# GpSimd's angles of the self-attention in the first attention stage instead of the second, their sine and cosine on ScalarE in the first stage's tail

## The reference

```python
x = x + _L0_xattn_ref(_layernorm(x), ctx_1024, W_q, b_q, W_kv, b_kv, W_o, b_o, pos_q, pos_k)
x = x + _L0_attn_ref(_layernorm(x), w_qkv, w_o, log_scale)
x = x + _L0_ffn_ref(_layernorm(x), router_w, router_bias, gate_w, up_w, down_w, ...)

def _L0_attn_ref(x, w_qkv, w_o, log_scale):
    ...
    scale = jnp.exp(log_scale)
    pos = jnp.arange(n, dtype=jnp.float32)
    theta = pos[None, None, :, None] * INV_FREQ[None, None, None, :] * scale[None, :, None, None]
    cos, sin = (jnp.cos(theta), jnp.sin(theta))
    q = _rotate(q, cos, sin)
    k = _rotate(k, cos, sin)
    ...
```

## Time and profile before

| | us |
|---|---|
| median of 3 runs (lowest, highest) | 1844.99 (1841.77, 1850.14) |
| the profiled execution | 1842.28 |
| its span, first to last instruction | 1840.8 |
| mean granted clock of TensorE | 0.968 |

### The profile page before, as it was taken

The page is one execution under the profiler, slowest core; times in us unless marked ns, Lnnn a source line. Parts: engine busy times, 40 slices in busy tenths (PEclk is TensorE's granted clock), DMA queues, the critical chain, the costliest instruction groups (busy, mean ns, idle before and its releaser), DMA issues.

```text
span 1840.8 us, 21317 instructions
## 1 busy us (share of the span) xinstructions
PE 1698.3 (92%) x8556; PEld 1131.3 (61%) x8556; DVE 1356.2 (74%) x1095; ACT 854.0 (46%) x1083; POOL 684.0 (37%) x323
## 2 busy tenths in 40 slices
PE   5589999999999996999999999999985998999998
PEld 4377777777777763333333333333565986888886
DVE  5579999999899997999898898898752553222222
ACT  3312222222222221877888888888731644333332
POOL 3266655666655653995000000000040004444442
PEclk7789999999999999999999999999997989999999
DMA  4634444344454338444444444455339003334441
GB/s 156 200 108 153 167 160 149 126 135 163 150 168 140 103 121 203 116 103 104 115 115 115 115 115 123 109 124 120 90 92 273 3 1 108 128 124 128 128 123 57
DMA packets 73905, 231.62 MB, mean 126 GB/s; under 512 B 8924, under 2 KB 9180, under 8 KB 62992
## 3 DMA queue, kind: packets, MB, share of 16 engines
q1 hardware_dynamic: 72768, 227.39, 42.8%
q10 hardware_dynamic: 1040, 2.88, 0.6%
HBM read 150.45 MB, written 59.84 MB: 114 GB/s over the span
## 4 chain that ended last, share of the span: by engine, by line
PE 56%; POOL 17%; DMA 8%; DVE 8%; issue 7%; ACT 4%; SPq 1%; POOLq 0%; ACTq 0%; DVEq 0%
PE PS L589 12%; PE PS L618 11%; PE PS L113 8%; PE PS L114 7%; PE PS L115 7%; DMA cs<-kr 6%; POOL kr L453 4%; POOL kr L450 4%; POOL cs L451 4%; POOL kl L464 4%; PE PS L371 3%; DVE mpart L375 2%; PE PS L871 2%; DVE acc L607 1%; PE PS L628 1%
## 5 line engine op out<-in xcount | busy, mean ns | idle before, releaser
L375 DVE TENSOR_REDUCE mpart<-PS 128x2 f32<-128x1024 f32 x512 | 584.3, 1220 | 57.0 <-PE PS L371 57.0
L607 DVE TENSOR_TENSOR acc<-acc,P 128x2048 f32<-128x2048 f32 x216 | 507.5, 2417 | 42.4 <-ACT P L595 42.4
L595 ACT ACTIVATE P<-PS 128x1024 f32<-128x1024 f32 x512 | 495.1, 1025 | 91.9 <-PE PS L589 66.7
L371 PE MATMUL PS<-kh,Qbd 128*128 128x512 f32 x1024 | 323.1, 397 | 25.6 <-ACT kh L462 13.1
L618 PE MATMUL PS<-P,qe 128*32 128x512 f32 x2048 | 272.9, 606 | 0.0
L371 PEld LDWEIGHTS PS<-kh,Qbd 128*128 128x128 f32 x1024 | 190.6, 190 | 82.5 <-DVE mpart L375 21.5
L108 POOL TENSOR_TENSOR w3l<-qk,w3h 128x2048 fp32r<-128x2048 f32 x2 | 9.1, 4564 | 491.5 <-ACT w3h L105 491.5
L108 POOL TENSOR_TENSOR El<-We,Eh 128x1536 fp32r<-128x1536 f32 x36 | 126.2, 3504 | 166.3 <-ACT Eh L105 166.3
L450 POOL TENSOR_TENSOR kr<-kr,cs 128x512 f32<-128x512 f32 x64 | 82.5, 1290 | 228.6 <-DMA cs<-kr 228.6
L1018 DVE TENSOR_TENSOR hf<-sg,PS 128x512 f32<-128x512 f32 x36 | 24.8, 688 | 192.8 <-PE PS L115 189.6
L438 ACT COPY cs<-PS 128x512 f32<-128x512 f32 x64 | 37.6, 590 | 239.8 <-PE PS L115 239.8
(11 more groups left out here) (206 smaller groups left out, 2734.4 us busy)
## 6 DMA issues: line engine op xcount, KB each, us to landing
kh<-kscr SPq DMA_DIRECT2D x129, 256.0 KB, 4.2
We<-in_w_e SPq DMA_DIRECT2D x36, 768.0 KB, 6.0
y<-in_y SPq DMA_DIRECT2D x16, 1024.0 KB, 4.8
cs<-kr SPq DMA_DIRECT2D x32, 512.0 KB, 6.3
vscr<-cs SPq DMA_DIRECT2D x16, 1024.0 KB, 4.3
kscr<-kh SPq DMA_DIRECT2D x16, 1024.0 KB, 4.3
kscr<-kl SPq DMA_DIRECT2D x16, 1024.0 KB, 4.3
qe<-vscr SPq DMA_DIRECT2D x64, 256.0 KB, 4.8
```

Of the source, the lines that this page charges most:

```text
L371: ins = nc.tensor.matmul(PS[:, 2 * b + t, :], Qbd[:, h, qt * 128:(qt + 1) * 128], kh[c % 2][:, g, :], start=True, stop=True)
L375: maxfree[b] = DV.sig(nc.vector.tensor_reduce(mpart[:, 4 * (h % 4) + g, 2 * qp:2 * qp + 2, c], PS[:, 2 * b:2 * b + 2, :], AX, ALU.max))
L595: expm[s, pr] = spfree[b] = AC.sig(nc.scalar.activation(P[s % 4][:, 2 * pr:2 * pr + 2, :], PS[:, 2 * b:2 * b + 2, :], ACT.Exp, scale=SCALE))
L607: accm[s] = DV.sig(nc.vector.tensor_tensor(a[:, :, :], a[:, :, :], P[s % 4][:, :, :], ALU.add))
```

## The change

The memory of `ang`, `nn`, `cosv` and `sinv` becomes one buffer `pool_of` of 6144. After chunk 0 has begun it holds `ks`, `vo` and the angles' three work tiles, so that `cs2` is free during the first stage. The exponential of the scales moves ahead of the first sines. The positions are loaded in iteration 0, behind the query's parts. GpSimd's operations are put in a list; `pr2` is computed in iteration 1, and after `rope_done` three operations of the list follow in each iteration from 1 on, until it is empty (thirteen times three and one). ScalarE takes the sines and cosines in the tail, and both old places disappear.

```diff
-        ks, vo = cs2[:, 0, :, :], [cs2[:, 1, :, :]]
+        pool_of = sbx("pool_of", [128, 6144])
+        ang, nn, cosv, sinv = [pool_of[:, 1536 * i:1536 * i + 1536] for i in range(4)]
+        ks, vo = [pool_of[:, 2048 * i:2048 * i + 2048].rearrange("p (g n) -> p g n", g=4) for i in range(2)]
+        pr2, tm2, n2 = [pool_of[:, 4096 + 512 * i:4608 + 512 * i] for i in range(3)]
+        ex = sbx("ex", [128, 4])
...
+        AC.wait(t_const)
+        t_ex = AC.sig(nc.scalar.activation(ex[:, :], cst[:, 4:8], ACT.Exp))
         AC.wait(t_ang)
...
+        angle_ops = []
+        for g in range(4):
+            a = cs2[:, 1, g, :]
+            angle_ops.append((nc.gpsimd.tensor_scalar, a, pr2, ex[:, g:g + 1], None, ALU.mult))
+            angle_ops.append((nc.gpsimd.tensor_scalar, n2, a, INV2PI, MAGIC, ALU.mult, ALU.add))
+            angle_ops.append((nc.gpsimd.tensor_scalar, n2, n2, MAGIC, None, ALU.subtract))
+            for part in (P2A, P2B, P2C):
+                angle_ops.append((nc.gpsimd.tensor_scalar, tm2, n2, part, None, ALU.mult))
+                angle_ops.append((nc.gpsimd.tensor_tensor, a, a, tm2, ALU.subtract))
+            angle_ops.append((nc.gpsimd.tensor_scalar, a, a, 3.1415925, -3.1415925, ALU.min, ALU.max))
+
+        def angles(n):
+            for _ in range(min(n, len(angle_ops))):
+                op, *args = angle_ops.pop(0)
+                t_ang2 = PL.sig(op(*args))
+                PL.wait(t_ang2)
+            return PL.last()
...
-                        AC.wait(v_out.get(c - 1))
+                        AC.wait(v_out.get(c - 1), t_cscr, t_qrot)
...
                         t_qbd, t_qout = query_parts()
+                        SP.wait(t_qrot, t_cscr)
+                        t_pos = l_a.dma(SP, n2, A["c_pos"].to_broadcast([128, 512]))
...
                 rope_done[c] = PL.sig(nc.gpsimd.tensor_tensor(kl[:, :, :], kr[:, :, :], ...
+                if c == 1:
+                    PL.wait(t_pos, t_ex, t_qrot, t_wks)
+                    PL.wait(PL.sig(nc.gpsimd.tensor_scalar(pr2, n2, cst[:, 2:3], None, ALU.mult)))
+                if c >= 1:
+                    t_ang2 = angles(3)
                 SP.wait(khm[c, 3])
...
                 for x in todo:
                     max_pair(*x)
+                AC.wait(t_ang2)
+                m = AC.sig(nc.scalar.activation(cs2[:, 0, :, :], cs2[:, 1, :, :], ACT.Abs))
+                AC.wait(m, t_eps)
+                AC.sig(nc.scalar.activation(cs2[:, 1, :, :], cs2[:, 1, :, :], ACT.Sin))
+                t_sin = AC.sig(nc.scalar.activation(cs2[:, 0, :, :], cs2[:, 0, :, :], ACT.Sin, scale=-1.0, bias=hpi[:, 0:1]))
...
-        t_pos = l_a.dma(SP, n2[:, :], A["c_pos"].to_broadcast([128, 512]))
-        t_ex = AC.sig(nc.scalar.activation(ex[:, :], cst[:, 4:8], ACT.Exp))
-        PL.wait(t_pos, t_ex, t_k1)
-        pool(nc.gpsimd.tensor_scalar(pr2[:, :], n2[:, :], cst[:, 2:3], None, ALU.mult))
-        for g in range(4):
...
-        AC.wait(t_ang2)
-        m = AC.sig(nc.scalar.activation(cs2[:, 0, :, :], cs2[:, 1, :, :], ACT.Abs))
-        AC.wait(m, t_eps)
-        AC.sig(nc.scalar.activation(cs2[:, 1, :, :], cs2[:, 1, :, :], ACT.Sin))
-        t_sin = AC.sig(nc.scalar.activation(cs2[:, 0, :, :], cs2[:, 0, :, :], ACT.Sin, scale=-1.0, bias=hpi[:, 0:1]))
```

More of the change, by code:

```diff
@@ L224, in build @@
         kr = sbx("kr", [128, 4, 512])
-        ks, vo = cs2[:, 0, :, :], [cs2[:, 1, :, :]]
         cs = [sbx(f"cs{i}", [128, 2, 512]) for i in range(2)]
[L227 to L232, removed]
+        pool_of = sbx("pool_of", [128, 6144])
[3 more added lines that the diff above has]
+        ex = sbx("ex", [128, 4])
+        wq, wk, wv, xn, qsw = y[0], cs2[:, 1, :, :], kr, cs2[:, 0, :, :], cs2[:, 0, :, :]
         xh, xl, wqh, wql = yh[1], yl[1], kh[1], kl
@@ L436, in build @@
                     else:
-                        AC.wait(v_out.get(c - 1))
-                        m = AC.sig(nc.scalar.copy(vo[0][:, :, (u - 4) * 128:(u - 3) * 128],
+                        AC.wait(v_out.get(c - 1), t_cscr, t_qrot)
+                        m = AC.sig(nc.scalar.copy(vo[:, :, (u - 4) * 128:(u - 3) * 128],
                                                   PS[:, 6 + b, :].rearrange("p (g n) -> p g n", g=4)))
@@ L455, in build @@
                         t_qbd, t_qout = query_parts()
+                        SP.wait(t_qrot, t_cscr)
+                        t_pos = l_a.dma(SP, n2, A["c_pos"].to_broadcast([128, 512]))
                     between()
                 SP.wait(vlast)
-                v_out[c] = l_vo.dma(SP, vscr[:, c].rearrange("g p n -> p g n"), vo[0][:, :, :])
+                v_out[c] = l_vo.dma(SP, vscr[:, c].rearrange("g p n -> p g n"), vo)
                 AC.wait(max_last.get(c - 2), kh_out.get(c - 2))
@@ L497, in build @@
         on = [sb2(f"on{i}", [128, 512]) for i in range(2)]
[L498 to L501, removed]
         for qt in range(4):
```

## The result

The changed kernel takes 1870.53 us (median of 4 runs, 1867.96 to 1871.79), the kernel before 1843.38 beside it; the ratio is 1.0139 with a 95% interval from 1.0110 to 1.0169. It is slower by 1.4%, near the forecast of 1873. Its profiled execution has a span of 1866.3 us, 25.5 more than before, and a mean granted clock of 0.958 (before 0.968).

| stretch (us) | before | after | difference |
|---|---|---|---|
| to the end of the last low keys | 693.2 | 732.8 | +39.6 |
| from there to the first score matmul of the second stage | 36.3 | 35.6 | -0.7 |
| first head group, to its denominators | 160.8 | 150.0 | -10.9 |
| the other three groups | 427.2 | 427.2 | 0 |
| from the last denominators to the end | 523.3 | 520.8 | -2.5 |

The account below looks back on a forecast made before the run. First stage bound by a ring of waits through the swap, second by TensorE and ScalarE in turn except at its start. 1842.3 + 40 - 11 = 1871.3 for the profiled execution; median 1873, range 1852 to 1900.

Parts of the forecast that it names:

- The ring and the hole: First stage: the chain low keys, swap, GpSimd rotation sets chunk length; GpSimd idles 12.96 us beside it, the transfers 1 us.
- The durations: Added GpSimd operations, first stage: 1.68, 0.75 and 1.40 us each with gaps, 52.9 us in the batches of chunks 1 to 12.
- The rival of short operations: GpSimd's one-input operations cost as little as 0.75 us, first-stage loss 22 us, time 1855; chance 0.14.
- The cost of a batch: First stage, chunks 2 to 13: each batch costs its length, about 4.4 us, minus the 1.05 us transfer hole; +40 us.
- The clock: TensorE, first stage: longer idling may halve its clock and issue the swap 2.3 us later; counted as nothing.
- the two delays run side by side: First stage: a swap issued 2.3 us later by the clock finds the transfer engines busy anyway; nothing added.
- the prediction's own sign of being wrong: First stage: the swap still landing 6.3 us after its issue with the `y` load late.
- The second stage: Removing GpSimd's 41 operations speeds VectorE's sums at the stage's start; -11 us, bounds 6 and 12.
- What was costed at nothing: Exponential, position load, tail sines, table loads and the third stage's cleared start: no gain or loss expected.
- the loads would be hidden: Rival, first stage: `y`, table and swap share the transfer engines without delaying the swap; 1833, chance 0.10.
- the delays would add: Rival, first stage: slower clock comes on top or mixing slows the swap more; 18 to 28 us more, 1896, chance 0.14.
- the balance: Rival, whole kernel: another split of the terms, such as half the queueing, gives within 9 us of now; 1845, chance 0.05.

## Why the prediction was right

The forecast was 1871.3 for the profiled execution and 1873 for the median; the profiled execution took 1867.96 (1866.3 from first to last instruction), the median is 1870.53.

**The ring and the hole.** Right. The batch did not touch the ring, GpSimd's idle time swallowed it, and the loss came by SP's wait and the order in the queue. Without the batch ahead of the low part of `y`, and separately with the swap ahead of the loads, the loss was gone.

**The durations.** Forecast were 1.57 us for a `tensor_scalar` of one operation, about 0.64 for one of two and 1.29 for two inputs. In the chunks the rows show 1.49 to 1.57, 0.62 and 1.27. The rival of short operations falls. The Trainium skill's 769 ns for 512 elements (GPSIMD Engine Reference, Elementwise — side-by-side cycle accounting) is met by neither kind; the row of before was the better guide.

**The cost of a batch.** The sum gave 40.2 us for twelve chunks; they cost 36.0 (12 x (41.95 - 38.95)), since `y` came 4.2 us later on average and not 4.4, and 1.2 of this was absorbed, not 1.05. To this come 3.5 us in chunks 14 and 15, where I had put nothing. In all 39.4 against 40.2: the total agrees partly because these two errors cancel.

**The clock.** The step "the two delays run side by side" held as a sum: in the nine of the twelve chunks in which the clock fell to half after the wait, the period was 40.2 to 42.6 us; in the three that kept it there, 44.5, 43.6 and 41.8. But the prediction's own sign of being wrong, a swap that lands 6.3 us after its issue with the `y` load late, did appear in chunks 5 and 11: there the swap, late with the clock, did not queue at all, and the clock's delay was the longer of the two. The step failed outright for chunks 14 and 15. There no load stood ahead of the swap, but TensorE still waited 2.69 and 1.97 us, its clock fell, and the swap was issued 1.6 us late; the run with ten small matmuls in the wait brought both back to 38.7. Before the change chunk 8 was of this kind too, with 40.2 us. Two others were longer for another reason: chunks 6 and 10 (40.1 and 39.3 us) kept the clock and issued the swap on time, but it took 7.79 and 7.04 us to land. The runs don't show what sets these off.

**The second stage.** Forecast -11 from bounds 9.4 and 12.1, measured -10.9 in the first group (160.8 to 150.0) and 0 in the others. The sums fell to 2.28 us.

**What was costed at nothing**, namely the exponential in the prologue, the sines in the tail, the table load and the third stage, was nothing, for the reasons given. That the loads would be hidden, or that the delays would add, did not happen, and the balance did not come about. But that the delays can add is shown by the run in which the load itself waited for the key tiles.

## What to carry to other kernels

An engine's idle time is only as free as the first thing that waits for what stands behind it in that engine's order. Before work is put into a hole, ask which result comes next on that engine, who waits for it, and what that waiter issues ahead of the critical transfer; here the exchange of two neighbours in GpSimd's order was worth 36 us. Where one queue carries both bulk loads and a transfer on which the ring waits, issue the latter first when it is ready at about the same time.

## What the runs showed of the hardware beyond the forecast

- On GpSimd a `tensor_scalar` of 512 fp32 per partition with one operation takes 1.49 to 1.57 us, with two operations 0.62, and a `tensor_tensor` 1.27.
- A transfer queued behind 1.5 MB on the same queue does not always run strictly after it: issued 1.3 us behind `y`, the swap landed 13.1 us after the issue of `y` (339.11 - 325.98), issued 3.3 us behind it, 11.3 us (255.27 - 243.99). The earlier issue landed later. In the changed kernel's twelve chunks with a `y` load, the three swaps issued up to 2.0 us behind `y` landed 12.1 to 13.1 us after it, the nine issued 3.3 to 4.8 us behind it 11.1 to 12.5. I have no run that tells why.
- SP's issue of `y` took 0.35 us where several microseconds had passed since its last issue, and 1.87 us right behind the swap.
